# A transformer kernel on one Trainium2 core: the score matmuls of a step issued in two halves

## The reference, cut to what matters

```
for i in range(DEPTH):                                   # 6 layers
    x = attn_layer(shift_tokens(x), Wqkv[i], q_scale[i], k_scale[i], Wo[i]) + x
    x = ffn_layer(shift_tokens(x), ln_g[i], ln_b[i], W1[i], b1[i], W2[i], b2[i]) + x
# attn_layer: 16 heads of 64 channels, windows of 32 tokens
q, k, v = split(x @ Wqkv)                                # 128 -> 3 x 1024
q, k = l2norm(q) * qs, l2norm(k) * ksc                   # then rotary tables on both
sim = einsum('bhwie,bhwje->bhwij', bq, bk2) * 8          # own window and the one before it
out = einsum('bhwij,bhwje->bhwie', softmax(masked sim), bv2)
return out.reshape(b, n, 1024) @ Wo
```

## Time and profile before

| | |
|---|---|
| time, median of 3 runs | 1795.9 us (1795.12 to 1799.96) |
| time of the profiled execution | 1795.17 us |
| its span, first to last instruction | 1793.4 us |
| busy share of the span | PE 90%, PEld 70%, DVE 82%, ACT 62%, POOL 55% |
| mean granted TensorE clock | 0.965 of full speed |

### The profile page before, as it was taken

How to read it: one execution, slowest core, us unless ns; L and a number is a source line. 1 busy time by engine, 2 the same in 40 slices (tenths; PEclk the granted TensorE clock), 3 DMA queues, 4 the chain that set the end, 5 groups by cost and what they waited for, 6 DMA issues and landing times. The chain is left out here.

```text
span 1793.4 us, 75405 instructions
## 1 busy us (share of the span) xinstructions
PE 1619.5 (90%) x31917; PEld 1247.0 (70%) x32013; DVE 1467.1 (82%) x3193; ACT 1106.4 (62%) x1990; POOL 992.7 (55%) x952
## 2 busy tenths in 40 slices
PE   5369999899999889999989999999999989999985
PEld 2147777677777767777767777767777767777762
DVE  8768888888888888888888888888888788888852
ACT  5236666566666656666656666666666656666652
POOL 2246646665555666555666546676556485565420
PEclk8579999999999999999999999999999999999998
DMA  3011111211101210111111111111101111011101
GB/s 100 26 51 36 39 28 31 77 32 36 50 24 36 61 46 27 47 36 36 56 42 38 47 36 35 52 46 39 47 24 39 59 47 39 24 47 39 36 14 48
DMA packets 40597, 74.95 MB, mean 42 GB/s; under 512 B 8992, under 2 KB 22088, under 8 KB 40264
## 3 DMA queue, kind: packets, MB, share of 16 engines
q1 hardware_dynamic: 40264, 70.11, 13.3%
HBM read 20.08 MB, written 2.10 MB: 12 GB/s over the span
## 5 line engine op out<-in xcount | busy, mean ns | idle before, releaser
L773 POOL TENSOR_TENSOR qk<-qk,qk_sin 128x512 f32<-128x512 f32 x384 | 490.9, 1278 | 217.0 <-DVE qk_sin L847 217.0
L781 POOL TENSOR_TENSOR qk<-qk,rnorm 128x512 f32<-128x512 f32 x384 | 400.4, 1043 | 371.7 <-DVE rnorm L884 371.7
L1024 ACT ACTIVATE squares<-bank 128x512 f32<-128x512 f32 x384 | 228.9, 596 | 168.2 <-DVE qk_sin L847 166.5
L1150 PE MATMUL bank<-w_hi,xs_hi 128*128 128x512 f32 x576 | 290.9, 505 | 14.0 <-ACT squares L1024 7.9
L857 DVE TENSOR_REDUCE norm<-squares 128x8 f32<-128x512 f32 x384 | 258.2, 677 | 30.7 <-ACT squares L1024 28.5
L841 DVE TENSOR_TENSOR qk<-bank,tables 128x512 f32<-128x512 f32 x384 | 261.5, 681 | 6.8 <-PE bank L1152 5.8
L847 DVE TENSOR_TENSOR qk_sin<-bank,tables 128x512 f32<-128x512 f32 x384 | 261.1, 680 | 0.0
L1160 PE MATMUL bank<-ident,qk 128*128 128x128 f32 x1536 | 236.5, 277 | 5.8 <-POOL qk L781 5.1
L1152 PE MATMUL bank<-w_hi,xs_lo 128*128 128x512 f32 x576 | 229.7, 399 | 0.0
L1151 PE MATMUL bank<-w_lo,xs_hi 128*128 128x512 f32 x576 | 228.3, 396 | 0.0
L1160 PEld LDWEIGHTS bank<-ident,qk 128*128 128x128 f32 x1536 | 184.8, 141 | 54.5 <-POOL qk L781 5.9
(11 more groups left out here) (161 smaller groups left out, 2588.1 us busy)
## 6 DMA issues: line engine op xcount, KB each, us to landing
v<-v SPq DMA_DIRECT2D x96, 390.0 KB, 3.5
v<-v SPq DMA_DIRECT2D x72, 130.0 KB, 3.4
w_raw<-in_L_ffn_Wqkv SPq DMA_DIRECT2D x36, 256.0 KB, 3.2
w_o_s<-in_L_ffn_Wo SPq DMA_DIRECT2D x6, 512.0 KB, 5.2
w_s<-in_L_ffn_W SPq DMA_DIRECT2D x6, 341.0 KB, 4.8
mix_x_nat<-in_L_attn_x SPq DMA_DIRECT2D x4, 256.0 KB, 3.7
x_res_scratch<-mix_x_res SPq DMA_DIRECT2D x4, 256.0 KB, 2.7
f_x_res<-x_res_scratch SPq DMA_DIRECT2D x4, 256.0 KB, 3.5
```

What stands on the lines that cost most here:

```text
L773: pool.tensor_tensor(qk[:, g % 2, c, :], qk[:, g % 2, c, :], qk_sin[:, c, :], ALU.add).then_inc(added[c], 1)
L781: pool.tensor_tensor(view, view, rnorm[:, g % 2, c * HPC:(c + 1) * HPC].unsqueeze(2) .to_broadcast([P, HPC, DH]), ALU.mult).then_inc(norme ...
L1024: act.activation(squares[:, c % 2, :], bank_of(Q0 + c)[:], ACT.Square).then_inc(squared[c], 1)
L1150: pe.matmul(bank_of(c)[:], l_hi, w_hi[:, cols], start=True, stop=False)
```

## The change

`score` is split in two functions: `open_scores` has the waits and the two mask matmuls, and `score(g, s)` issues one half of the 128 score matmuls (64 for each value of `s`; the same matmuls in the same order). The calls become `open_scores`, `score(.., 0)`, `turn_o(.., 1)`, `project(.., K0)`, `score(.., 1)`, `project(.., K1)`. The semaphore `scored` is still raised by the last two matmuls of the second half. Nothing is added or removed, and no other engine's list changes. From line 1194 of the kernel before on, line numbers in the changed kernel are 4 higher.

```diff
-            def score(g, step):
+            def open_scores(g, step):
                 if not live(g):
                     return
...
                 for r in range(2):
                     pe.matmul(bank[4 + r][:], ident_bf[:], mask_bf[:, min(g % NBLK, 1), :], start=True, stop=True)
+
+            def score(g, s):
+
+                if not live(g):
+                    return
                 tok = P * (g % NBLK)
-                for s in range(2):
-                    for place in range(NWIN):
+                for place in range(NWIN):
+                    w = 2 * (place % 2) + place // 2
+                    col = (NWIN * s + place) * 2 * WINDOW
+                    for h in range(4):
+                        pair = 4 * s + h
...
+                            if s == 1 and place == NWIN - 1 and h == 3:
+                                mm.then_inc(scored, 1)
...
                 turn_o(step - 3, 0)
-                score(step - 2, step)
+                open_scores(step - 2, step)
+                score(step - 2, 0)
                 turn_o(step - 3, 1)
                 project(step, K0)
+                score(step - 2, 1)
                 project(step, K1)
```

More of the change, by code:

```diff
@@ L1184, in score @@
                     pe.matmul(bank[4 + r][:], ident_bf[:], mask_bf[:, min(g % NBLK, 1), :], start=True, stop=True)
+            def score(g, s):
+                if not live(g):
+                    return
                 tok = P * (g % NBLK)
-                for s in range(2):
-                    for place in range(NWIN):
[L1188 to L1199, removed]
+                for place in range(NWIN):
[3 more added lines that the diff above has]
+                        pair = 4 * s + h
+                        for r in range(2):
+                            row = slice(DH * r, DH * (r + 1))
+                            mm = pe.matmul(bank[4 + r][WINDOW * h:WINDOW * (h + 1), col:col + 2 * WINDOW],
+                                           q_t[row, pair, WINDOW * w:WINDOW * (w + 1)],
+                                           k_t[row, pair, tok + WINDOW * w:tok + WINDOW * w + 2 * WINDOW],
+                                           start=False, stop=True, skip_group_check=True)
+                            if s == 1 and place == NWIN - 1 and h == 3:
+                                mm.then_inc(scored, 1)
             def turn_probs(g, r):
```

## The result

The changed kernel takes 1885.91 us (median of 4 runs, 1880.28 to 1887.35), the kernel before 1795.51 (4 runs): a ratio of 1.0497, 95% interval 1.0464 to 1.0531. That is 90 us, where 62 were forecast, and above the range's end of 1884. The profiled execution is at 1880.28, with a span of 1878.5.

The account below looks back on a forecast made before the run. PE and DVE were taken as near their limit, with hardly any slack between them after the scores. Delay of +116.4 us less 52.6 of holes gave +63.8 on 1795.2: 1859, taken as 1858 us, range 1828 to 1884.

Parts of the forecast that it names:

- The delay is paid 96 times, the hole is earned 52 times and only up to the delay's own size: Score bursts: later last scores cost 116.4 us over 96 steps; shrinking holes in 52 bursts give back 52.6 us.
- The delay: Last score of a whole burst: 1.40 us later, from transposes 0.41, `K0` 0.78 and passages 0.11 and 0.09.
- the step on merge_heads: PE after the scores: merge_heads now waits for DVE's shift and starts 1.15 us later, 1.40 less 0.25.
- the 64 of the sum: Whole program: net loss of 63.8 us, from 116.4 us of delay less 52.6 us of holes given back.
- there merge_heads' 1.15 counts: Steps with `t` = 0, 1 and 3: slack at `V1` leaves merge_heads' lateness of 1.15 us as the loss, 72 times.
- `V1` late by 1.40 everywhere: Variant of the likeliest case: `V1` 1.40 us late in every step, 134 - 53 = +82 us, 1877 us.
- DVE's wait: DVE's maximum waiting for the scores: from 95 us before to some 170 us after.
- The wait of merge_heads: merge_heads (L1265) newly waiting for DVE's shift in every step: 0.9 to 1.15 us each, 90 to 110 us in all.
- The faster one: Rival: holes hidden, DVE chain has slack, PE alone counts, gaining 52.6 us and paying 19: 1762 us; chance 0.06.
- No hole is shortened: Rival: holes in the score bursts keep their size, so the whole 116 us stays: 1911 us; chance 0.07.
- Nothing comes of it: Rival: later shift and square are made up further on, holes and delay cancel: 1796 us; chance 0.05.
- the smaller loss: Rival: some steps absorb the delay (at `t` = 0 and 1), say half of the 60: 1805 to 1830 us; chance 0.07.

Follow-up runs that it names:

- three lengths of the insertion: Changed kernel's split with only the four transposes of o between the halves, 1834.65 us; with only `K0` between, 1855.89 us; with both (the change), 1885.91 us.
- the run with the late maximum: Kernel before, unsplit, with DVE's first maximum waiting in addition for the end of `K0`, so DVE starts 1.33 us later: 1914.62 us, ratio 1.0666.
- the shifted packets: Kernel before with 48 idle transposes (96 instructions) on PE ahead of the first step: 1791.67 us, one run.
- The run with the wait put last: Changed kernel with merge_heads waiting for `x1_done` first and for `shifted[0]` last: 1881.96 us, ratio to the kernel before 1.0467.

## Why the prediction was wrong in size, by its own steps

**The mechanism and the sign.** "The delay is paid 96 times, the hole is earned 52 times and only up to the delay's own size" is what happened. The table above follows this sum for three lengths of the insertion, and the run with the late maximum shows the delay by itself. The holes are borders of packets (the shifted packets show it) and do shrink by the inserted work: 50.9 us gone, 52.6 forecast. The Trainium skill (Runtime: NRT & Kernel Launch, Instruction fetch mechanics) says that crossing a block of instructions is mostly hidden. This trace does not agree: crossing one in a dense burst costs up to 3.4 us here, in 52 bursts of 96. It does agree with the skill's blocks of 256.

**The delay**, forecast 1.40, was 1.45: 96 x 0.05 = 5 us. The passage out of the scores is 0.15 us from the last score to the transpose, not 0.11.

**The step that failed** is the one on merge_heads: "It could start 0.3 us after the shift and needs about 0.05, as at `V1`; so it now waits for the shift, and starts 1.40 - 0.25 = 1.15 us later than before." The way from the shift to merge_heads takes 0.26, so the slack was 0.04 and not 0.25; and even the 0.04 does not reach `V1`, which is late by the full 1.45 at every `t`. So 72 x 0.25, some 18 us, were credited that don't exist: with the 5 us of the delay nearly all of what lies between the 64 of the sum and the 88 below. I had taken the release from another wait (ACT to PE, one semaphore) instead of leaving it open. The run with the wait put last found 0.11 us of it in one more wait behind the decisive one; what the other 0.15 consists of stays open. The sentence "there merge_heads' 1.15 counts" was incomplete besides: at `t` = 0 and 3 the expansion and the variance wait for the residual, later on DVE's chain. In the kernel before it ends 0.27 us ahead of their weight load, and the way takes 0.12, so that path had 0.15 of slack and would by itself have left 1.30 of the 1.45.

With 1.45 in place of 1.15 and 1.40, the sum is 96 x 1.45 less 50.9 = 88 us. That is 1883 on the profiled execution's time before, and 1880.3 was measured in the profiled one of after. The difference is the 6.8 us of the late merge_heads, given back, less 4 us lost in small amounts elsewhere. The other three runs are 5 to 7 us higher than the profiled one. The range had named the case ("`V1` late by 1.40 everywhere", 1877) and stopped 7 us above it, less than the spread between runs.

**What was to be seen.** DVE's wait: 170 us forecast, 181.0 measured. The wait of merge_heads: 90 to 110 forecast, 86.1 on PE and 107.1 on its weight loads. `V1` waits for the squares at `t` = 2: yes. The issue wait ahead of the scores below 30 us: no for PEld (85.6), since each of two entries into small tiles idles a little; yes for PE (5.4). 12.9 us of holes are left in all, where 9 were forecast.

**The rivals.** The faster one needed over 1.2 us of slack, and there are 0.04. "No hole is shortened" falls with 50.9 us gone. "Nothing comes of it" and the smaller loss fall with the unchanged ways from last score to `V1`: no kind of step absorbs anything in the median, and the nine late steps gave back 6.8 us, where the smaller loss needed some 30.

## What to carry to other kernels

Before work is moved into a stall, ask who waits for what stands behind the stall: if that is the chain that sets the end, filling the hole earns nothing by itself, and in every pass without a hole the filling is pure delay. Where two engines run almost in step, take each slack as zero until the release time of that very wait has been read, and look for all semaphores through which the late chain comes back, not for the first. A stall that comes from dense instructions is better thinned by moving dense stretches apart where nothing is delayed.

## What the runs showed of the hardware

- A burst of 256 PE instructions in 1.3 us outruns the arrival of its instructions. Of 96 bursts 52 are cut by 0.1 to 3.4 us at a border of 256 instructions; with 96 instructions more ahead of the loop the cuts moved by 48 scores. PE resumes 2.3 to 2.9 us after the packet's start.
- Right behind the three holes of 2.7 us and more (those that begin at 598.07, 1142.38 and 1416.72) the granted clock was about 0.5 of full speed, and merge_heads came 0.9 to 1.6 us later than usual.
- 64 by 32 tiles that take the two row halves of the array, and two banks, in turn start every 10.2 ns, and every 14.0 ns when all use the same half and the same bank.
- The way from DVE's write to a PE instruction with five waits takes 0.25 us; with the decisive wait last, 0.14.
